# Second attention: row maxima turned in two halves, and only the first half ahead of the first score

## Chip, cores and metric

The kernel runs on one core of one Trainium2 chip. The metric is the device time of one execution in microseconds; three runs of the kernel before gave 2145.66, 2147.05 and 2149.94 us, median 2147.05. A difference of about 0.2% (4.3 us) is what a measurement of this kernel can tell from none.

## What is computed

Two transformer layers with adaptive layer norm. Each is an attention and a feed-forward part with a gated residual. Only the second layer's attention is touched: 32 heads of 16 dimensions, one key and one value head shared by all of them, causal, for 2 batches of 1024 tokens:

```python
q = (x @ wq).reshape(B, T, N_HEADS, HEAD_DIM)
k = x @ wk
v = x @ wv
scores = jnp.einsum('bqhd,bkd->bhqk', q, k) * scale
scores = jnp.where(causal[None, None], scores, -jnp.inf)
probs = jax.nn.softmax(scores.astype(jnp.float32), axis=-1)
out = jnp.einsum('bhqk,bkd->bqhd', probs, v).reshape(B, T, C)
```

The softmax subtracts the row maximum, which the kernel computes in a pass of its own.

## The kernel before

`attention1` is one block in which every engine runs its own written-out program; semaphores alone order them. It has 16 **steps** (`STEPS1`), one for each batch and group of 4 heads (`G`). A step has 12 **sets** (`QUADS`), the pairs of a half of the queries (`qc`, 512 of them) and a tile of 128 keys (`kt`) that the causal mask leaves: sets 0 to 3 belong to the first half of the queries, sets 4 to 11 to the second. In a set TensorE forms 4 score tiles, or 2 where two heads share one (sets 2, 3, 10 and 11), in three PSUM banks `scp` (`score`, L1770); ScalarE takes the exponential of each into `prob` (L1663). After each odd set TensorE multiplies the probabilities of two earlier sets with the values (`values`, L1817).

The negated row maximum enters a score as one more row of the queries (`MAXROW`), against a row of ones in the keys. So before a step's first score its maxima must be known. They come from a second pass over the same scores, in **units** (`maximum`, L1787 and L1792): a unit is 128 queries of a pair of heads against up to 512 keys, in one of two double banks `mxp`; VectorE reduces it (L1711 for a full unit, L1713 for one with the diagonal). A step has 24 units. Units 0 to 7 are the first four query tiles (256, 256, 512, 512, ... up to 1024 elements a row for both heads); units 8 to 23 the other four tiles, each with a full unit and a diagonal unit for both pairs of heads. After unit 23 VectorE joins the two parts (L1717). Then `turn_maxima` (L1805) transposes all maxima of the step on TensorE into the next `mxp` bank, ScalarE negates them into `mrow` (L1676), and SyncE moves them with 2 DMAs into the `MAXROW` rows of the step's query tile (L1612).

The order is written in numbers. 32 units (`LEAD`: the whole of step 0 and eight of step 1) and the turn of step 0 stand ahead of the first score. Then every set brings two units (`MQUAD`), so that step t's maxima are finished in set 7 of step t-1. They are turned at set 9 (`TURN_AT`), and TensorE waits for the row at set 0 of step t. A bank of `mxp` is free for its next user when VectorE has reduced the unit in it, or ScalarE has copied the turned maxima out of it (`freed`). In the last step no units are left, and `unread` (L1800) puts two matmuls that nobody reads in the place of each.

Of the kernel before, what the change touches and what calls it, by code (L numbers as in the profile page):

```python
# [17 lines left out]
P = 128  # L18
# [7 lines left out]
G = 4  # L26
# [1072 lines left out]
ATT1 = ("q_in2 q_in3 m_in0 m_in1 m_in2 m_in3 sc_ready exp_done pv_done u_copied mx_ready mx_done mx_joined "  # L1099
# [466 lines left out]

def max_banks():


    order = [("max", u) for u in range(LEAD)] + [("turn", 0)]  # L1570
    for q in range(QSETS):
        if q % QUADS == TURN_AT and q // QUADS + 1 < STEPS1:
            order.append(("turn", q // QUADS + 1))
        order += [("max", u) for u in range(LEAD + MQUAD * q, min(LEAD + MQUAD * (q + 1), MSTEP * STEPS1))]
    return {what: (i % MXBANKS, order[i - MXBANKS] if i >= MXBANKS else None) for i, what in enumerate(order)}


def attention1(nc, k, q_dram, sums, recips, stale, queries_in, next_loads, closed):

    with ExitStack() as ctx:  # L1580
# [5 lines left out]
        mxd, mxf = sb("mxd", [P, 2, 2, PAIRS, TILES]), sb("mxf", [P, 2, 2, PAIRS, TILES // 2])  # L1586
        mrow = sb("mrow", [G * TILES, 2, P], F32R)
# [5 lines left out]
        q_in, m_in = [s[f"q_in{i}"] for i in range(SLOTS1)], [s[f"m_in{i}"] for i in range(SLOTS1)]  # L1593
        MOVES = 16 * 3 * 2
        banks = max_banks()
        def freed(eng, what):
            before = banks[what][1]
            if before is not None and before[0] == "max":
                eng.wait_ge(s["mx_done"], before[1] + 1)
            if before is not None and before[0] == "turn":  # L1600
                eng.wait_ge(s["mrow_done"], before[1] + 1)

        with nc.Block() as block:
            @block.sync
            def _(sp):
# [27 lines left out]
                move(2)  # L1633
                next_loads(sp)
                maxima_row(0)
                for t in range(STEPS1):
                    if t >= 1:
                        if t + 3 < STEPS1:
                            sp.wait_ge(s["sc_ready"], SCORES1 * t)
                            move(t + 3)  # L1640
                        results(t - 1)
                    elif t + 3 < STEPS1:
                        move(t + 3)
                    if t + 1 < STEPS1:
                        maxima_row(t + 1)
                    if t >= 1:
                        reciprocals(t - 1)
# [4 lines left out]
            def _(act):  # L1652
# [19 lines left out]
                def maxima_out(t):  # L1672
                    act.wait_ge(s["mt_ready"], t + 1)
                    if t >= 2:
                        act.wait_ge(m_in[(t - 2) % SLOTS1], 32 * ((t - 2) // SLOTS1 + 1))
                    nc.scalar.activation(mrow[:, t % 2, :], mxp[banks["turn", t][0]][0:G * TILES, 0, 0:P], ACT.Copy, scale=-1.0).then_inc(s["mrow_done"], 1)  # L1676
                maxima_out(0)
                for t in range(STEPS1):
                    for n in range(QUADS):
                        if n == TURN_AT and t + 1 < STEPS1:  # L1680
                            maxima_out(t + 1)
# [21 lines left out]
            def _(dve):  # L1703
                def maximum(u):
                    t, (i, qt, part) = u // MSTEP, MPAIRS[u % MSTEP]
                    if u % MSTEP == 0 and t >= 2:
                        dve.wait_ge(s["mt_ready"], t - 1)
# [27 lines left out]
                for u in range(LEAD):  # L1735
                    maximum(u)
                for g in range(QSETS):
                    for u in range(LEAD + MQUAD * g, min(LEAD + MQUAD * (g + 1), MSTEP * STEPS1)):
# [9 lines left out]
            def _(pe):  # L1748
# [53 lines left out]
                def turn_maxima(t):  # L1802
                    pe.wait_ge(s["mx_joined"], t + 1)
                    freed(pe, ("turn", t))
                    nc.tensor.transpose(mxp[banks["turn", t][0]][0:G * TILES, 0, 0:P], mxd[:, t % 2].rearrange("p j i q -> p (j i q)"),  # L1805
# [379 lines left out]
```

## Time and profile before

| | us |
|---|---|
| median of 3 runs | 2147.05 |
| the profiled execution | 2148.23 |
| its span, first to last instruction | 2146.4 |
| TensorE busy in the span | 1964.6 (92%) |
| VectorE busy | 1174.6 (55%) |
| ScalarE busy | 903.1 (42%) |
| second attention, first unit to last values | 1462.9 to 2019 |

The profile's page gives busy times over the whole program. The second attention is read from its own windows and timelines. A window's row gives busy time for each engine and the mean clock granted to TensorE as a share of 2.4 GHz (0.50 is 1.2 GHz). Timelines give each instruction's start and length, and in brackets how long the engine sat idle before it and on whom. Matmuls overlap, so their lengths don't add up; distances between starts do.

### The profile page before, as it was taken

How to read it: one execution, taken by the hardware profiler on the slowest of the kernel's cores; microseconds unless marked ns; L12 is line 12 of the kernel's file. 1: busy time of each engine (PE TensorE's matmuls, PEld its weight loads, DVE VectorE, ACT ScalarE, POOL GpSimd, SP SyncE). 2: the span in 40 equal slices, each digit the busy share in tenths (PEclk: the TensorE clock that was granted, in tenths of full speed). 3: DMA queues.
4: the chain of work that ended last, by engine and by line, in shares of the span. 5: the costliest groups of instructions: out<-in, count | busy, mean ns of one | idle time of the engine just before them, and what ended most of it. 6: DMA issues, size and time to landing. Idle time of an engine off the chain costs nothing. (4 is left out here: it accounts for less than half of the span.)

```text
span 2146.4 us, 34674 instructions
## 1 busy us (share of the span) xinstructions
PE 1964.6 (92%) x12824; PEld 1177.3 (55%) x12824; DVE 1174.6 (55%) x2557; ACT 903.1 (42%) x1909; POOL 524.5 (24%) x408
## 2 busy tenths in 40 slices
PE   4859999999999999999986899997999999999698
PEld 4635666666666666666643454553444444444377
DVE  3536655555555555555401454446676767765078
ACT  2513344444444444444440122221666656656444
POOL 0014245555434444555330000000000000000143
PEclk8969999999999999999998999996999999999799
DMA  9742233222333233322236221144132222210121
GB/s 308 272 143 60 61 80 81 62 58 58 76 81 80 71 80 80 80 60 57 66 93 198 69 69 48 51 111 134 22 53 42 38 52 39 42 37 19 33 88 59
DMA packets 113594, 172.21 MB, mean 80 GB/s; under 512 B 26186, under 2 KB 46826, under 8 KB 113298
## 3 DMA queue, kind: packets, MB, share of 16 engines
q1 hardware_dynamic: 112402, 169.75, 29.8%
q8 instruction: 101, 1.65, 0.3%
q14 instruction: 67, 0.55, 0.1%
q10 hardware_dynamic: 1024, 0.26, 0.1%
HBM read 84.32 MB, written 29.38 MB: 53 GB/s over the span
## 5 line engine op out<-in xcount | busy, mean ns | idle before, releaser
L890 ACT ACTIVATE at_prob<-at_scp 128x512 f32<-128x512 f32 (+1 forms) x608 | 349.8, 576 | 515.4 <-PE at_scp L993 514.4
L1663 ACT ACTIVATE as_prob<-as_scp 128x512 f32<-128x512 f32 (+2 forms) x640 | 308.7, 564 | 197.5 <-PE as_scp L1773 148.2
L925 DVE CUSTOM_DVE_ANT_0 at_junk<-at_mxp,causal 128x128 f32<-128x128 f32 (+3 forms) x512 | 243.5, 488 | 190.5 <-PE at_mxp L1004 185.7
L1713 DVE TENSOR_REDUCE as_mxd<-as_mxp 128x2 f32<-128x256 f32 (+3 forms) x256 | 202.6, 820 | 98.3 <-PE as_mxp L1792 96.1
L920 DVE TENSOR_REDUCE at_mxf<-at_mxp 128x1 f32<-128x512 f32 x256 | 176.0, 688 | 143.4 <-PE at_mxp L1004 139.6
L1698 POOL TENSOR_TENSOR l_att_t<-l_att_t,as_spread 64x1024 f32<-64x1024 f32 x16 | 37.9, 2368 | 860.3 <-DMA as_spread<-l_recips 860.3
L820 POOL TENSOR_TENSOR at_pre<-at_prob 128x512 f32<-128x512 f32 x64 | 80.1, 1281 | 410.6 <-ACT at_prob L890 410.6
L1711 DVE TENSOR_REDUCE as_mxf<-as_mxp 128x2 f32<-128x1024 f32 x128 | 151.0, 1221 | 52.8 <-PE as_mxp L1787 52.6
L820 POOL TENSOR_TENSOR at_pre<-at_pre,at_prob 128x512 f32<-128x512 f32 x128 | 160.5, 1284 | 3.6 <-ACT at_prob L890 1.2
L1817 PE MATMUL as_op<-as_prob,l_vn 128*32 128x512 f32 (+3 forms) x1536 | 158.1, 533 | 0.3 <-ACT as_u_sb L1670 0.3
L989 PE MATMUL at_scp<-hd_early_q,l_khi 97*128 97x512 f32 (+1 forms) x304 | 138.3, 455 | 11.3 <-DMA hd_late_q<-at_slo 8.2
L1026 PE MATMUL at_op<-at_prob,l_cn 128*32 128x512 f32 (+3 forms) x1536 | 144.4, 493 | 4.0 <-ACT at_u_sb L861 4.0
L989 PE MATMUL at_scp<-at_qhi,l_khi 97*128 97x512 f32 (+1 forms) x304 | 138.7, 456 | 0.8 <-ACT at_prob L890 0.5
L1004 PE MATMUL at_mxp<-l_khi,hd_early_q 96*128 96x512 f32 (+2 forms) x384 | 126.2, 383 | 10.5 <-DMA hd_early_q<-at_shi 9.3
L1004 PE MATMUL at_mxp<-l_khi,at_qhi 96*128 96x512 f32 (+2 forms) x384 | 122.5, 367 | 0.5 <-DVE at_tm L950 0.2
L992 PE MATMUL at_scp<-hd_late_q,l_khi 96*128 96x512 f32 (+1 forms) x304 | 118.0, 388 | 0.0
L993 PE MATMUL at_scp<-hd_early_q,l_klo 96*128 96x512 f32 (+1 forms) x304 | 117.7, 387 | 0.0
L992 PE MATMUL at_scp<-at_qlo,l_khi 96*128 96x512 f32 (+1 forms) x304 | 116.8, 384 | 0.0
L993 PE MATMUL at_scp<-at_qhi,l_klo 96*128 96x512 f32 (+1 forms) x304 | 116.3, 383 | 0.0
L1787 PE MATMUL as_mxp<-l_keys,hd_early_q 48*128 48x512 f32 (+2 forms) x384 | 97.7, 488 | 19.2 <-DVE as_mxf L1711 7.3
L1770 PE MATMUL as_scp<-as_q,l_keys 49*128 49x512 f32 (+2 forms) x320 | 105.3, 444 | 7.4 <-ACT as_prob L1663 5.9
L1770 PE MATMUL as_scp<-hd_early_q,l_keys 49*128 49x512 f32 (+2 forms) x320 | 103.6, 445 | 5.7 <-ACT as_prob L1663 4.3
(250 smaller groups left out, 3494.4 us busy)
## 6 DMA issues: line engine op xcount, KB each, us to landing
hd_late_q<-at_slo SPq DMA_DIRECT2D x96, 128.0 KB, 2.4
at_qhi<-at_shi SPq DMA_DIRECT2D x96, 128.0 KB, 2.5
at_qlo<-at_slo SPq DMA_DIRECT2D x96, 128.0 KB, 2.4
hd_early_q<-at_shi SPq DMA_DIRECT2D x84, 128.0 KB, 2.4
at_spread<-l_recips SPq DMA_DIRECT2D x64, 128.0 KB, 2.7
l_o<-at_u_sb SPq DMA_DIRECT2D x16, 512.0 KB, 3.4
hd_early<-in_wmod SPq DMA_DIRECT2D x7, 1024.0 KB, 6.8
hd_late<-l_o SPq DMA_DIRECT2D x12, 512.0 KB, 4.1
```

The costliest lines, as they stand in the source:

```text
L820: nc.gpsimd.tensor_tensor(pre[:, j, :], other, prob[:, (x + j) % RING0, :], ALU.add).then_inc(s["pre_done"], 1)
L890: nc.scalar.activation(prob[:, x % RING0, c0:HALF], scp[x % BANKS0][:, c0:HALF], ACT.Exp).then_inc(s["exp_done"], 1)
L920: nc.vector.reduce_max(mxf[:, j, qt - 4:qt - 3], tile[:], AX_X).then_inc(s["mx_done"], 1)
L925: nc.vector.tensor_tensor_reduce(out=junk[:, u % 2, 0:w], in0=tile[:, 0:w], in1=k.causal[:, HALF - w:HALF], scale=1.0, scalar=LOWEST, op0= ...
L989: nc.tensor.matmul(out, k.khi[0:KR + 1, b, ks], q_cols(qhi[t % 2][0:KR + 1]), start=True, stop=False)
L992: nc.tensor.matmul(out, k.khi[0:KR, b, ks], q_cols(qlo[t % 2][0:KR]), start=False, stop=False)
L993: nc.tensor.matmul(out, k.klo[0:KR, b, ks], q_cols(qhi[t % 2][0:KR]), start=False, stop=True).then_inc(s["sc_ready"], 1)
L1004: nc.tensor.matmul(bank("max", t, u)[:, 0:w], qhi[t % 2][0:KR, qt // 4, j, qt % 4 * P:(qt % 4 + 1) * P], k.khi[0:KR, t // NG, k0:k0 + w], ...
L1663: nc.scalar.activation(prob[:, x % RING1, cols], scp[x % BANKS1][:, cols], ACT.Exp).then_inc(s["exp_done"], 1)
L1713: nc.vector.reduce_max(mxd[:, t % 2, :, i, qt:qt + 1], tile[:, :, 0:(qt % 4 + 1) * P], AX_X).then_inc(s["mx_done"], 1)
L1770: mm = nc.tensor.matmul(out, k.keys[rows, t // NG, kt * P:(kt + 1) * P], queries, start=True, stop=not diagonal)
L1817: mm = nc.tensor.matmul(op[2 * HD * j:2 * HD * (j + 1), c0:HALF], k.vn[:, t // NG, kt, :], prob[:, (x + j % UNITS1_OF[n]) % RING1, p0:p0 + ...
```

## The change

The 24 units keep their order. Only units 0 to 7 stand ahead of the first score; the turn, the negated copy and the move into the query tile are done for each half of the query tiles on its own. The first half's turn waits for eight units and stands at set 8 of the step before (`TURN_A1`); the second half's waits for the join and stands at set 1 of its own step, at set 3 in step 0 (`TURN_B1`). TensorE waits for a step's first half row at set 0, for its second half row at set 4. The lead over the sets shrinks from 32 units to 22. In step 0, sets 0, 1 and 2 carry 6, 6 and 8 units. A half row takes 4 DMAs of 4 x 128 elements, so a step has 8 in place of 2. On SyncE's queue the first half row goes ahead of the loads for the closing part (`next_loads`), and the second half row ahead of the results of the step before. In the last step `unread` begins at set 3.

```diff
-MPAIRS = [(i, qt, part) for qt in range(TILES) for part in range(1 + qt // 4) for i in range(PAIRS)]
+MPAIRS = [(i, qt, part) for half in range(2) for qt in range(4 * half, 4 * half + 4) for part in range(1 + half) for i in range(PAIRS)]
-LEAD = MSTEP + 8
-TURN_AT = 9
+FIRST_PAIRS = 4 * PAIRS
+LEAD = 22
+TURN_A1, TURN_B1 = 8, (3, 1)
...
+def pairs_ahead(g):
+    return FIRST_PAIRS + 6 * g if g < 3 else min(LEAD + MQUAD * g, MSTEP * STEPS1)
+
+def turns1(t, n):
+    return [(t, 1)] * (n == TURN_B1[min(t, 1)]) + [(t + 1, 0)] * (n == TURN_A1 and t + 1 < STEPS1)
...
-                def maxima_row(t):
-                    sp.wait_ge(s["mrow_done"], t + 1)
+                def maxima_row(t, half):
+                    sp.wait_ge(s["mrow_done"], 2 * t + half + 1)
                     for jj in range(2):
-                        sp.dma_start(words(q[t % SLOTS1][RG * jj + MAXROW:RG * jj + MAXROW + 1, :, :]),
-                                     words(mrow[jj * G * TILES // 2:(jj + 1) * G * TILES // 2, t % 2, :])).then_inc(m_in[t % SLOTS1], 16)
+                        for i in range(PAIRS):
+                            r = (jj * PAIRS + i) * TILES // 2
+                            sp.dma_start(words(q[t % SLOTS1][RG * jj + MAXROW:RG * jj + MAXROW + 1, i, HALF * half:HALF * (half + 1)]),
+                                         words(mrow[r:r + TILES // 2, t % 2, half, :])).then_inc(row_in[half][t % SLOTS1], 16)
...
                 move(2)
+                maxima_row(0, 0)
                 next_loads(sp)
-                maxima_row(0)
                 for t in range(STEPS1):
+                    if t >= 1 and t + 3 < STEPS1:
+                        sp.wait_ge(s["sc_ready"], SCORES1 * t)
+                        move(t + 3)
+                    maxima_row(t, 1)
                     if t >= 1:
-                        if t + 3 < STEPS1:
-                            sp.wait_ge(s["sc_ready"], SCORES1 * t)
-                            move(t + 3)
                         results(t - 1)
                     elif t + 3 < STEPS1:
                         move(t + 3)
                     if t + 1 < STEPS1:
-                        maxima_row(t + 1)
+                        maxima_row(t + 1, 0)
...
-                def turn_maxima(t):
-                    pe.wait_ge(s["mx_joined"], t + 1)
-                    freed(pe, ("turn", t))
+                def turn_maxima(t, half):
+                    if half == 0:
+                        pe.wait_ge(s["mx_done"], MSTEP * t + FIRST_PAIRS)
+                    else:
+                        pe.wait_ge(s["mx_joined"], t + 1)
+                    freed(pe, ("turn", t, half))
...
-                for u in range(LEAD):
+                for u in range(FIRST_PAIRS):
                     maximum(u)
-                turn_maxima(0)
+                turn_maxima(0, 0)
                 for g in range(QSETS):
                     t, n = divmod(g, QUADS)
-                    if n == TURN_AT and t + 1 < STEPS1:
-                        turn_maxima(t + 1)
-                    if n == 0:
-                        pe.wait_ge(m_in[t % SLOTS1], 32 * (t // SLOTS1 + 1))
-                    mine = range(LEAD + MQUAD * g, min(LEAD + MQUAD * (g + 1), MSTEP * STEPS1))
+                    for which in turns1(t, n):
+                        turn_maxima(*which)
+                    if n % 4 == 0 and n < 8:
+                        pe.wait_ge(row_in[n // 4][t % SLOTS1], ROWS * (t // SLOTS1 + 1))
+                    mine = range(pairs_ahead(g), pairs_ahead(g + 1))
                     for i in range(MQUAD):
-                        for u in mine[i:i + 1]:
+                        for u in mine[i * len(mine) // MQUAD:(i + 1) * len(mine) // MQUAD]:
                             maximum(u)
-                        if t == STEPS1 - 1:
-                            if n == 0 and i == 0:
+                        if t == STEPS1 - 1 and n >= 3:
+                            if n == 3 and i == 0:
                                 pe.wait_ge(s["mx_done"], MSTEP * STEPS1)
-                                pe.wait_ge(s["mrow_done"], STEPS1)
+                                pe.wait_ge(s["mrow_done"], 2 * STEPS1)
                             unread(t)
```

TensorE around the first turn and the first scores, of the kernel before (L1787 and L1792 are a unit, L1805 the turn, L1770 to L1773 a score; `hd_early_q` holds the queries):

```order
L1787 MATMUL as_mxp<-l_keys,hd_early_q 128x512 x2
L1792 MATMUL as_mxp<-l_tri 128x128 x4
L1805 MATMUL as_mxp<-ident,as_mxd 32x128
L1787 MATMUL as_mxp<-l_keys,hd_early_q 128x512 x2
L1770 MATMUL as_scp<-hd_early_q,l_keys 128x512
L1772 MATMUL as_scp<-l_tri 128x128
L1773 MATMUL as_scp<-l_tri 128x128
```

And of the changed kernel (L1805 and L1810 are a unit there, L1826 the turn, L1788 to L1791 a score):

```order
L1805 MATMUL as_mxp<-l_keys,hd_early_q 128x512 x2
L1810 MATMUL as_mxp<-l_tri 128x128 x4
L1826 MATMUL as_mxp<-ident,as_mxd 16x128
L1805 MATMUL as_mxp<-l_keys,hd_early_q 128x512 x4
L1805 MATMUL as_mxp<-l_keys,hd_early_q 128x256 x2
L1810 MATMUL as_mxp<-l_tri 128x128 x4
L1788 MATMUL as_scp<-hd_early_q,l_keys 128x512
L1790 MATMUL as_scp<-l_tri 128x128
L1791 MATMUL as_scp<-l_tri 128x128
```

The turn has 8 units ahead of it in place of 32 and takes half the columns; three units stand between it and the first score in place of one.

TensorE from the second unit of set 0 to the first of set 1 in a later step, before:

```order
L1787 MATMUL as_mxp<-l_keys,as_q 128x512 x2
L1770 MATMUL as_scp<-hd_early_q,l_keys 128x512
L1772 MATMUL as_scp<-l_tri 128x128
L1773 MATMUL as_scp<-l_tri 128x128
L1770 MATMUL as_scp<-hd_early_q,l_keys 128x512
L1772 MATMUL as_scp<-l_tri 128x128
L1773 MATMUL as_scp<-l_tri 128x128
L1787 MATMUL as_mxp<-l_keys,as_q 128x256 x2
L1792 MATMUL as_mxp<-l_tri 128x128 x4
```

The same place in the changed kernel:

```order
L1805 MATMUL as_mxp<-l_keys,hd_early_q 128x512 x2
L1810 MATMUL as_mxp<-l_tri 128x128 x4
L1788 MATMUL as_scp<-hd_early_q,l_keys 128x512
L1790 MATMUL as_scp<-l_tri 128x128
L1791 MATMUL as_scp<-l_tri 128x128
L1788 MATMUL as_scp<-hd_early_q,l_keys 128x512
L1790 MATMUL as_scp<-l_tri 128x128
L1791 MATMUL as_scp<-l_tri 128x128
L1826 MATMUL as_mxp<-ident,as_mxd 16x128
L1805 MATMUL as_mxp<-l_keys,as_q 128x256 x2
L1810 MATMUL as_mxp<-l_tri 128x128 x4
```

Set 0 now carries units 22 and 23, which have the diagonal, and the second half's turn stands between its last score and set 1, straight behind the unit whose reduction it waits for.

SyncE's queue up to the second row of maxima, before (L1120 loads queries, L1857 to L1862 are `next_loads`, L1612 is the row):

```order
L1120 DMA as_q<-scratch_queries 16x2x1024 x6
L1857 DMA hd_late<-in_wo 128x4x512
L1858 DMA hd_late<-scratch_w_feed 128x4x512
L1859 DMA l_bias<-in_b_base 128x512
L1862 DMA l_gates<-gate_rows 128x512 x4
L1612 DMA hd_early_q<-as_mrow 1x16x128 x2
L1120 DMA as_q<-scratch_queries 16x2x1024 x6
L1612 DMA hd_early_q<-as_mrow 1x16x128 x2
```

And of the changed kernel (L1627 is a half row):

```order
L1121 DMA as_q<-scratch_queries 16x2x1024 x6
L1627 DMA hd_early_q<-as_mrow 1x4x128 x4
L1878 DMA hd_late<-in_wo 128x4x512
L1879 DMA hd_late<-scratch_w_feed 128x4x512
L1880 DMA l_bias<-in_b_base 128x512
L1883 DMA l_gates<-gate_rows 128x512 x4
L1627 DMA hd_early_q<-as_mrow 1x4x128 x4
L1121 DMA as_q<-scratch_queries 16x2x1024 x6
L1627 DMA hd_early_q<-as_mrow 1x4x128 x4
```

The half row stands ahead of the closing part's loads, in 4 DMAs in place of 2.

## Rows read from the trace of the kernel before

**Rows 1.** Windows: us; busy us (x) of PE, PEld, DVE, ACT, POOL; clock; DMA.

```profile
1462.90:1494.50 31.60, 25.79 (x160) 13.54 (x160) 27.17 (x33) 0.00 (x0) 0.00 (x0) 0.50 0.48 134
...
1497.70:1509.80 12.10, 12.06 (x84) 7.61 (x84) 7.02 (x8) 5.93 (x12) 0.00 (x0) 0.52 0.35 65
...
1629.70:1661.30 31.60, 29.78 (x301) 15.40 (x297) 23.13 (x29) 20.21 (x43) 1.24 (x1) 1.00 0.24 41
1661.30:1694.60 33.30, 31.50 (x301) 15.60 (x297) 23.20 (x29) 20.20 (x43) 3.60 (x2) 0.95 0.27 47
1974.80:1984.20 9.40, 8.67 (x75) 3.80 (x71) 0.00 (x0) 5.53 (x13) 0.00 (x0) 1.00 0.14 35
```

**Rows 2.** Timeline of VectorE before the first score: start us, us, what.

```profile
1468.99 2.36 DVE L1713 TENSOR_REDUCE as_mxd<-as_mxp 128x2 f32<-128x1024 f32 x2 [0.27 <-PE as_mxp L1792]
...
1493.17 2.36 DVE L1713 TENSOR_REDUCE as_mxd<-as_mxp 128x2 f32<-128x1024 f32 x2 [0.27 <-PE as_mxp L1792]
```

**Rows 3.** Timeline of all engines, first turn of the maxima to the first score.

```profile
1494.54 0.37 PE L1805 MATMUL as_mxp<-ident,as_mxd 128*32 128x128 f32 x1 [0.55 <-DVE as_mxd L1713]
...
1495.24 1.17 SPq L1612 DMA_DIRECT2D hd_early_q<-as_mrow  x2
...
1497.72 0.80 PE L1787 MATMUL as_mxp<-l_keys,hd_early_q 48*128 48x512 f32 x2 [2.81 <-DMA hd_early_q<-as_mrow]
```

**Rows 4.** Groups of one shape over the second attention: busy us, mean ns, idle before.

```profile
L1711 DVE TENSOR_REDUCE as_mxf<-as_mxp 128x2 f32<-128x1024 f32 x128 | 151.0, 1221 | 52.8 <-PE as_mxp L1787 52.6
...
L1713 DVE TENSOR_REDUCE as_mxd<-as_mxp 128x2 f32<-128x1024 f32 x64 | 75.1, 1216 | 0.5 <-PE as_mxp L1792 0.5
L1713 DVE TENSOR_REDUCE as_mxd<-as_mxp 128x2 f32<-128x768 f32 x64 | 58.3, 952 | 34.5 <-PE as_mxp L1792 34.5
...
L1713 DVE TENSOR_REDUCE as_mxd<-as_mxp 128x2 f32<-128x512 f32 x64 | 43.3, 689 | 17.9 <-PE as_mxp L1792 15.8
...
L1713 DVE TENSOR_REDUCE as_mxd<-as_mxp 128x2 f32<-128x256 f32 x64 | 27.1, 423 | 45.4 <-PE as_mxp L1792 45.3
```

**Rows 5.** Timeline of TensorE: set 8 of step 4, sets 0 to 3 of step 5.

```profile
1650.37 0.38 PE L1787 MATMUL as_mxp<-l_keys,as_q 48*128 48x256 f32 x2
...
1661.35 0.50 PE L1787 MATMUL as_mxp<-l_keys,as_q 48*128 48x512 f32 x2
...
1663.17 0.38 PE L1787 MATMUL as_mxp<-l_keys,as_q 48*128 48x256 f32 x1
...
1665.30 0.86 PE L1817 MATMUL as_op<-as_prob,l_vn 128*32 128x256 f32 x16
1666.09 0.50 PE L1787 MATMUL as_mxp<-l_keys,as_q 48*128 48x512 f32 x2
...
1667.91 0.39 PE L1787 MATMUL as_mxp<-l_keys,as_q 48*128 48x256 f32 x2 [0.61 <-DVE as_mxf L1711]
...
1669.48 1.71 PE L1817 MATMUL as_op<-as_prob,l_vn 128*32 128x512 f32 x16
```

**Rows 6.** Timeline of VectorE, step 5: units 8 and 9, then 22, 23 and the join.

```profile
1661.89 2.36 DVE L1711 TENSOR_REDUCE as_mxf<-as_mxp 128x2 f32<-128x1024 f32 x2 [0.53 <-PE as_mxp L1787]
...
1678.60 2.35 DVE L1713 TENSOR_REDUCE as_mxd<-as_mxp 128x2 f32<-128x1024 f32 x2
1680.97 0.18 DVE L1717 TENSOR_TENSOR as_mxd<-as_mxd,as_mxf 128x16 f32<-128x16 f32 x1
```

**Rows 7.** Timeline of TensorE, last step: set 2 and the values after set 3.

```profile
1988.79 0.39 PE L1800 MATMUL as_mxp<-l_keys,as_q 48*128 48x256 f32 x2
...
1991.46 1.71 PE L1817 MATMUL as_op<-as_prob,l_vn 128*32 128x512 f32 x16 [0.34 <-ACT as_u_sb L1670]
```

**Rows 8.** Windows: dense stretch at the start, and around one fall of the clock.

```profile
1502.00:1508.00 6.00, 5.99 (x45) 4.05 (x45) 4.11 (x5) 3.38 (x8) 0.00 (x0) 0.50 0.01 3
...
1676.00:1680.00 4.00, 3.66 (x24) 1.90 (x22) 3.68 (x4) 3.51 (x9) 0.00 (x0) 0.99 0.00 0
1680.00:1683.00 3.00, 3.00 (x17) 0.59 (x16) 1.12 (x2) 1.12 (x3) 0.00 (x0) 0.50 0.00 0
```

More of the change, by code:

```diff
@@ L1564, in _ @@
                             split_keys(g)
+def pairs_ahead(g):
+    return FIRST_PAIRS + 6 * g if g < 3 else min(LEAD + MQUAD * g, MSTEP * STEPS1)
+def turns1(t, n):
+    return [(t, 1)] * (n == TURN_B1[min(t, 1)]) + [(t + 1, 0)] * (n == TURN_A1 and t + 1 < STEPS1)
 def max_banks():
-    order = [("max", u) for u in range(LEAD)] + [("turn", 0)]
+    order = [("max", u) for u in range(FIRST_PAIRS)] + [("turn", 0, 0)]
     for q in range(QSETS):
-        if q % QUADS == TURN_AT and q // QUADS + 1 < STEPS1:
-            order.append(("turn", q // QUADS + 1))
-        order += [("max", u) for u in range(LEAD + MQUAD * q, min(LEAD + MQUAD * (q + 1), MSTEP * STEPS1))]
+        order += [("turn", *which) for which in turns1(*divmod(q, QUADS))]
+        order += [("max", u) for u in range(pairs_ahead(q), pairs_ahead(q + 1))]
     return {what: (i % MXBANKS, order[i - MXBANKS] if i >= MXBANKS else None) for i, what in enumerate(order)}
@@ L1592, in attention1 @@
         op = ps("op", [P, HALF])
-        q_in, m_in = [s[f"q_in{i}"] for i in range(SLOTS1)], [s[f"m_in{i}"] for i in range(SLOTS1)]
+        q_in = [s[f"q_in{i}"] for i in range(SLOTS1)]
+        row_in = [[s[f"{name}{i}"] for i in range(SLOTS1)] for name in ("m_in", "m_late")]
+        ROWS = 16 * 2 * PAIRS
         MOVES = 16 * 3 * 2
@@ L1600, in freed @@
             if before is not None and before[0] == "turn":
-                eng.wait_ge(s["mrow_done"], before[1] + 1)
+                eng.wait_ge(s["mrow_done"], 2 * before[1] + before[2] + 1)
         with nc.Block() as block:
@@ L1670, in copy_out, with maxima_out @@
                     nc.scalar.activation(u_sb[:, t % 2, HALF * hf:HALF * (hf + 1)], op[:], ACT.Copy).then_inc(s["u_copied"], 1)
-                def maxima_out(t):
-                    act.wait_ge(s["mt_ready"], t + 1)
+                def maxima_out(t, half):
+                    act.wait_ge(s["mt_ready"], 2 * t + half + 1)
                     if t >= 2:
-                        act.wait_ge(m_in[(t - 2) % SLOTS1], 32 * ((t - 2) // SLOTS1 + 1))
-                    nc.scalar.activation(mrow[:, t % 2, :], mxp[banks["turn", t][0]][0:G * TILES, 0, 0:P], ACT.Copy, scale=-1.0).then_inc(s["mrow_done"], 1)
-                maxima_out(0)
+                        act.wait_ge(row_in[half][(t - 2) % SLOTS1], ROWS * ((t - 2) // SLOTS1 + 1))
+                    nc.scalar.activation(mrow[:, t % 2, half, :], mxp[banks["turn", t, half][0]][0:G * TILES // 2, 0, 0:P], ACT.Copy, scale=-1.0).then_inc(s["mrow_done"], 1)
+                maxima_out(0, 0)
                 for t in range(STEPS1):
                     for n in range(QUADS):
-                        if n == TURN_AT and t + 1 < STEPS1:
-                            maxima_out(t + 1)
+                        for which in turns1(t, n):
+                            maxima_out(*which)
                         exps(t, n)
@@ L1706, in maximum @@
                     if u % MSTEP == 0 and t >= 2:
-                        dve.wait_ge(s["mt_ready"], t - 1)
+                        dve.wait_ge(s["mt_ready"], 2 * t - 3)
+                    if u % MSTEP == FIRST_PAIRS and t >= 2:
+                        dve.wait_ge(s["mt_ready"], 2 * t - 2)
                     tile = mxp[banks["max", u][0]]
@@ L1734, in split_weights @@
                     nc.vector.tensor_tensor(low[:, c, :], whole[:, c, :], high[:, c, :].bitcast(F32), ALU.subtract).then_inc(s["w_lo"], 1)
-                for u in range(LEAD):
+                for u in range(FIRST_PAIRS):
                     maximum(u)
                 for g in range(QSETS):
-                    for u in range(LEAD + MQUAD * g, min(LEAD + MQUAD * (g + 1), MSTEP * STEPS1)):
+                    for u in range(pairs_ahead(g), pairs_ahead(g + 1)):
                         maximum(u)
@@ L1800, in unread @@
                         nc.tensor.matmul(tile[:, jj, 0:2 * P], q[t % SLOTS1][rows, 0, 0:P], k.keys[rows, t // NG, 0:2 * P], start=True, stop=True)
[L1802 to L1805 removed]
+                def turn_maxima(t, half):
[4 more added lines that the diff above has]
+                    freed(pe, ("turn", t, half))
+                    nc.tensor.transpose(mxp[banks["turn", t, half][0]][0:G * TILES // 2, 0, 0:P], mxd[:, t % 2, half].rearrange("p j i q -> p (j i q)"),
                                         k.ident[:]).then_inc(s["mt_ready"], 1)
```

14 lines of the change are left out of this document (7 added, 7 removed).

## The prediction

> **What bounds the kernel now.** I read the windows of the second attention first. A whole step of 31.6 us (step 4) has TensorE busy for 29.78, VectorE for 23.13, ScalarE for 20.21, at clock 1.00; step 5 took 33.3 us at 0.95 [rows 1]. So in the steps TensorE is the bound by its own order, with short waits on the two others. Ahead of them lies a stretch of another kind: for 34.8 us (1462.9 to 1497.7) no score is formed. In its first 31.6 us VectorE is busy for 27.17 and the clock is 0.50 [rows 1]; the last 3 us go to the turn and the row. The reader is to see that VectorE reducing 32 units sets the pace there. Next I read when unit 7 is reduced (1468.99 + 2.36 = 1471.35, for units 6 and 7 together) and when the last of the lead is (1495.53) [rows 2], and the chain from the turn to the first score: turn at 1494.54, two DMAs issued from 1495.24 to 1496.41, TensorE going on at 1497.72, so 0.70 us to the issue, 0.585 for each DMA and 1.31 after the last [rows 3].
>
> **The head.** The first turn can start when unit 7 is reduced, at about 1471.4. The issue starts at 1472.1; four DMAs take 4 x 0.585 = 2.34 instead of 1.17, and 1.31 more lands the half row at 1475.8, against 1497.7. This is no gain of 22 us, since 24 units are only moved behind it. Sets 0 to 2 carry 20 units, 8 to 27. VectorE needs for them 8 x 1.221 for the full ones, 2 x (1.216 + 0.952 + 0.689 + 0.423) = 6.56 for the diagonal ones of the second half, 0.18 for the join and 2 x (0.423 + 0.689) = 2.22 for units 24 to 27, together 18.7 us [rows 4]. It was busy for 27.17 of 31.60 us in the lead, 88% after the first 0.9 us; at that share the 18.7 take 21.2 us, and with the first unit coming at 1476.5 they end at 1497.7. The ten scores of these sets fit beside. TensorE may begin set 3 a little sooner, near 1497.2. Sets 0 to 3 with their values took 12.1 us before at clock 0.52 [rows 1]; set 3 and the values are about 5 of it. Set 4 then begins at 1502.2 in place of 1509.8: a gain of 7.6 us. The second half row, turned at the start of set 3, lands 0.70 + 2.34 + 1.31 = 4.4 us later, just under those 5. Bounds: 5.5 (the waits of both engines add up more than in the lead, or the row is late) and 9.5 (the clock rises before set 3, and only the row, at about 1501, is waited for).
>
> **Steps 1 to 14, sets 0 and 1.** Here is what the change adds each time. Units 22 and 23 now stand in set 0, and the second half's turn right behind it; it waits for the join. Queued behind it on TensorE are units 0 and 1 and the four scores of set 1, and ScalarE, which has done set 0 by then, waits for these. In step 5 set 0 began at 1661.35 and set 1 at 1663.17, 1.82 us later [rows 5]. VectorE began the first of set 0's units 0.54 after its start and needed 2.35 for units 22 and 23 together, then 0.18 for the join [rows 6]. With the diagonal's matmuls 0.1 later this gives 0.64 + 2.35 + 0.18 = 3.2 us after the set's start. TensorE has its four scores by 2.1 (1.82 and two diagonals), so it stands for 1.1 us, and with 0.2 for the turn set 1 begins at 3.4 instead of 1.82: 1.6 late. Set 1 took 2.13 (to 1665.30) [rows 5], partly behind the exponentials of set 0, which no longer queue: 0.4 back. I take +1.2. Bounds +0.4 (only the turn and the diagonals, if the reductions are further ahead than in this row) and +1.6.
>
> **Sets 2 and 3** take from 1666.09 to 1669.48, 3.39 us, of which TensorE waits 0.61 for the reduction of a full unit [rows 5]. They now carry units 2 to 5, whose reductions take 0.42 to 0.95. The nearest row is the last step, in which unread matmuls stand there: from 1988.79 to 1991.46, 2.67 us, ended by the copy of the output on ScalarE [rows 7]. I take -0.7; the bounds are 0 and -0.8.
>
> **The other sets.** Full and diagonal units change places. In sets 4 to 9 the exponentials of 4 x 512 columns pace the scores, and a diagonal costs 0.1 where it comes ahead of the first score. Sets 10 and 11 win about 0.1 by full units. The first half's turn stands at set 8 with 6 later units behind its last one, so nothing waits. Together 0, between -0.2 and +0.3. The DMAs: 8 for 2 is 3.5 us of issue a step on SyncE. The half row for set 4 is issued at the start of set 1 and needs 4.4 us; sets 1 to 3 with values take over 6. Were that cover gone, TensorE would stand at set 4 for what is over. The results behind it on the queue wait for the output copy of set 2 anyway, the other half row has sets 8 to 11 (11 us), and the query load stands ahead as before. All nothing.
>
> A step is so 1.2 - 0.7 = +0.5 us, 14 steps +7.0, with bounds -0.3 and +1.5 for one step.
>
> **The end.** Sets 8 to 11 of step 14 had no units and took 9.4 us (1974.8 to 1984.2) [rows 1]; with units they take 1661.35 - 1650.37 = 11.0 [rows 5]: +1.6. Step 15 pays the wait of set 0 (+1.2) and saves at most 0.2 where sets 0 to 2 lose their unread matmuls: +1.0. Bounds for both 1.5 and 4, since without unread matmuls the clock may fall sooner.
>
> **Sum.** -7.6 + 7.0 + 1.6 + 1.0 = +2.0 us on the profiled execution's 2148.23, so 2150.2. That execution is 1.2 above the median of the runs, so 2149.0.
>
> **The clock.** Fine windows show seven stretches at half clock in steps 1 to 14, one in every second step: after 4 us in which TensorE was busy for 3.66, the next 3 us ran at 0.50 [rows 8]. One costs 1.7 us (33.3 against 31.6) [rows 1]. I leave their number at seven. But sets 6 and 7, behind which they fall, now stream fewer columns (units 10 to 13 instead of 20 to 23), and the new stand in set 0 is a second weak place.
> The Trainium skill (TensorE: Matmul & The Clock Gate, What's actually happening) says that the clock drops after an idle window and rises under sustained matmuls. The trace does not agree: here it fell after a stretch without such a gap, and in the head it stayed at 0.50 through 6.00 us of which TensorE was busy for 5.99 [rows 8]. By the page a stand of 1.1 us adds no fall, the sum stays at 2149, and the denser head would rise early, which would give 2147.
>
> **Rivals.**
> *The steps come out even or better* (27%). TensorE stands behind ScalarE in most sets, so part of the 1.2 us may be won back in sets 1 to 3. At 0 a step the sum is 2142, at -0.3 and a head of 9.5 it is 2136. For it: VectorE has 8.5 us free a step. Against: the join can't come before two reductions of 1.2 us that start in set 0.
> *More falls of the clock* (20%), slower. If the weak place of set 6 and 7 or of set 0 is met in every step, seven further stretches at 1.7 us add 12: 2161; three add 5: 2154. It decides from two on. For it: fewer columns there, and a stand; against: the falls came only in every second step.
> *The wait is dearer* (14%), slower. If VectorE enters set 0 with unit 21 undone, or nothing comes back in sets 1 to 3, a step costs +1.3: 14 x 0.8 = 11 more, 2160. It decides from +0.7 a step.
> *The change doesn't shorten the head* (3%): if the row or VectorE makes sets 0 to 3 as long as the lead was, +8: 2157.
> My own sum has 36%.
>
> **The numbers.** 0.2%, 4.3 us, is about what a measurement of this kernel can tell from none. My sum and the smaller versions of the rivals lie inside 2142.8 to 2151.3. Faster: 0.28, nearly all of it the first rival. Slower: 0.35, the second, third and fourth less their mild forms, with a part of mine. Same: 0.37. The range is 2139 to 2161: it leaves out the best head with gaining steps, and the clock together with a dear wait. The likeliest case alone has 2144 to 2154.
>
> **What would show it.** In the new trace: the first score within 1478 to 1480 (right) and set 4 of step 0 near 1502; a wait of TensorE on the join of about 1 us before 15 of the second turns; sets 2 and 3 in about 2.7 us; half-clock stretches in every second step. I am wrong if that wait is under 0.4 or over 1.6, if set 4 begins outside 1500 to 1505, or if the clock falls in most steps.

## The result, and the profile after

The changed kernel takes 2170.96 us (median of 4 runs, 2169.97 to 2172.64) against 2146.36 for the one before (4 runs): ratio 1.0117, 95% interval 1.0105 to 1.0129. It is 24.6 us slower. The forecast was 2149.0 with a range of 2139 to 2161; the time lies outside it.

Four windows of the second attention tell where the time went: to set 4 of step 0, the rest of step 0, steps 1 to 14, step 15. Their columns are those of [rows 1]. Before the change:

```profile
1462.90:1509.80 46.90, 38.23 (x245) 21.25 (x245) 35.22 (x41) 7.48 (x14) 0.00 (x0) 0.51 0.42 107
1509.80:1531.60 21.80, 20.97 (x203) 10.42 (x199) 15.20 (x17) 14.27 (x30) 0.00 (x0) 1.00 0.06 15
1531.60:1984.20 452.60, 426.85 (x4116) 215.54 (x4112) 312.27 (x372) 282.93 (x602) 30.83 (x13) 0.97 0.23 40
1984.20:2018.90 34.70, 32.94 (x252) 16.21 (x248) 0.35 (x1) 19.86 (x42) 4.72 (x2) 0.80 0.09 17
```

After it:

```profile
1461.40:1500.50 39.10, 30.08 (x204) 15.96 (x204) 26.22 (x31) 7.48 (x15) 0.00 (x0) 0.50 0.43 118
1500.50:1525.70 25.20, 24.69 (x187) 11.81 (x183) 15.54 (x16) 14.29 (x30) 0.00 (x0) 0.78 0.18 28
1525.70:2003.90 478.20, 448.55 (x4176) 224.59 (x4172) 322.09 (x381) 285.48 (x616) 31.41 (x14) 0.95 0.22 38
2003.90:2042.20 38.30, 36.06 (x253) 16.86 (x249) 3.03 (x5) 20.38 (x43) 4.12 (x2) 0.73 0.08 16
```

| part (to the hundredth from the timelines) | before | after | change |
|---|---|---|---|
| first unit to set 4 of step 0 | 46.87 | 39.11 | -7.8 |
| sets 4 to 11 of step 0 | 21.72 | 25.21 | +3.5 |
| steps 1 to 14 | 452.6 | 478.2 | +25.6 |
| step 15 to the end of its values | 34.8 | 38.3 | +3.5 |

The head gave what was forecast (7.6), and steps 1 to 14 gave back more than three times as much. The four changes add up to +24.9 us; the two traced executions are 23.0 us apart (spans of 2169.4 and 2146.4), since the attention began 1.6 us earlier and what follows it took 0.3 us less. The head's chain, a timeline of all engines, answers to [rows 3]:

```profile
1469.78 0.38 PE L1826 MATMUL as_mxp<-ident,as_mxd 128*16 128x128 f32 x1 [1.59 <-DVE as_mxd L1731]
...
1470.49 2.54 SPq L1627 DMA_DIRECT2D hd_early_q<-as_mrow  x4
...
1474.11 1.22 PE L1805 MATMUL as_mxp<-l_keys,hd_early_q 48*128 48x512 f32 x4 [3.95 <-DMA hd_early_q<-as_mrow]
...
1476.81 0.77 PE L1788 MATMUL as_scp<-hd_early_q,l_keys 49*128 49x512 f32 x2
```

The turn comes at 1469.78 (the attention begins at 1461.36 here, 1.6 us earlier than in the trace before), the half row takes four DMAs in 2.54 us, TensorE stands for 3.95 us, and the first score is formed at 1476.81, 15.5 us after the first unit instead of 35.

One step, TensorE's timeline, set 0 to the values after set 3 (answers to [rows 5]):

```profile
1696.52 0.49 PE L1805 MATMUL as_mxp<-l_keys,as_q 48*128 48x512 f32 x2
...
1699.81 0.28 PE L1826 MATMUL as_mxp<-ident,as_mxd 128*16 128x128 f32 x1 [0.89 <-DVE as_mxd L1735]
1700.01 0.39 PE L1805 MATMUL as_mxp<-l_keys,as_q 48*128 48x256 f32 x2
...
1702.02 0.86 PE L1838 MATMUL as_op<-as_prob,l_vn 128*32 128x256 f32 x16
1702.80 0.39 PE L1805 MATMUL as_mxp<-l_keys,as_q 48*128 48x256 f32 x2
```

```profile
1705.66 1.71 PE L1838 MATMUL as_op<-as_prob,l_vn 128*32 128x512 f32 x16
```

and VectorE's beside it (answers to [rows 6]):

```profile
1697.18 2.36 DVE L1731 TENSOR_REDUCE as_mxd<-as_mxp 128x2 f32<-128x1024 f32 x2 [0.53 <-PE as_mxp L1810]
1699.58 0.18 DVE L1735 TENSOR_TENSOR as_mxd<-as_mxd,as_mxf 128x16 f32<-128x16 f32 x1
```

The turn at 1699.81 has waited 0.89 us for the join of 1699.58. The chain is the forecast one: the step's units 22 and 23 are reduced in 2.36 us from 1697.18 on, and nothing else can go in front. It stands in all 15 of these turns (13.2 us in total, 0.88 or 0.89 each). Sets 0 and 1 took 5.50 us (1696.52 to 1702.02) against 3.95, sets 2 and 3 2.86 (1702.80 to 1705.66) against 3.39.

Steps 1 to 13 of the kernel before took 33.25 and 31.63 us in turn (within 0.01), the longer ones with one stretch at half clock. After the change each of the fourteen takes 34.13 to 34.17 us, and each has such a stretch, behind sets 6 and 7. Windows around one:

```profile
1679.00:1682.00 3.00, 2.31 (x12) 0.99 (x9) 2.14 (x3) 3.00 (x7) 0.00 (x0) 1.00 0.00 0
1682.00:1686.00 4.00, 4.00 (x18) 0.83 (x18) 0.65 (x1) 1.38 (x3) 0.00 (x0) 0.57 0.00 0
```

TensorE was busy for 2.31 of the 3.00 us ahead of the fall: in sets 6 and 7 it stands behind ScalarE, and its units there are now small (10 and 11 have 256 keys).

### The profile page after: what moved, and what is told of

Read it like the earlier page. It is cut to its first block and busy times, and to the rows that moved or that the text cites. A ratio compares the mean times of both kernels' runs of the same rounds, so it can differ in the third digit from the quotient of the medians.

```text
span 2169.4 us, 34858 instructions
## 1 busy us (share of the span) xinstructions
PE 1983.1 (91%) x12828; PEld 1180.3 (54%) x12828; DVE 1178.9 (54%) x2557; ACT 906.1 (42%) x1925; POOL 524.6 (24%) x408
## 5 line engine op out<-in xcount | busy, mean ns | idle before, releaser
L1838 PE MATMUL as_op<-as_prob,l_vn 128*32 128x512 f32 (+3 forms) x1536 | 172.7, 575 | 2.1 <-ACT as_u_sb L1686 0.8
L1788 PE MATMUL as_scp<-as_q,l_keys 49*128 49x512 f32 (+2 forms) x320 | 115.4, 465 | 7.1 <-ACT as_prob L1679 5.9
L1788 PE MATMUL as_scp<-hd_early_q,l_keys 49*128 49x512 f32 (+2 forms) x320 | 114.2, 471 | 6.1 <-ACT as_prob L1679 5.0
L1805 PE MATMUL as_mxp<-l_keys,hd_early_q 48*128 48x512 f32 (+2 forms) x384 | 101.3, 474 | 13.7 <-PEq L1220 4.7
```

What stands on the lines that cost most here:

```text
L1788: mm = nc.tensor.matmul(out, k.keys[rows, t // NG, kt * P:(kt + 1) * P], queries, start=True, stop=not diagonal)
L1838: mm = nc.tensor.matmul(op[2 * HD * j:2 * HD * (j + 1), c0:HALF], k.vn[:, t // NG, kt, :], prob[:, (x + j % UNITS1_OF[n]) % RING1, p0:p0 + ...
```

## The experiments

Every run has its median beside the kernel before on the same chip. For steps 1 to 14 I also give what a full step without half clock in it takes (the **clean step**; those of one trace agree within 0.05), and what the fourteen took over 14 clean steps (the **clock's cost**). A **fall** is a stretch at half clock. The clock's cost comes from one traced execution for each kernel. Before: 31.63 us, and 452.6 + 1.6 (step 14 lacked eight units) - 442.8 = 11.4. After: no step is clean. The runs were made on three chips, on which the kernel before took 2147.03, 2147.47 and 2146.47 us, so medians of different chips can be set side by side to about 1 us.

The theories: the **stand** (the wait on the join is a loss in every step), **columns** (the clock falls because sets 6 and 7 now stream fewer of them), and **length** (the clock falls at intervals that the length of a step decides).

**1. The second turn one set later.**

```diff
-TURN_A1, TURN_B1 = 8, (3, 1)
+TURN_A1, TURN_B1 = 8, (3, 2)
```

> The changed kernel with the second half's turn at set 2 instead of set 1 (step 0 stays at set 3); all else the same. Three theories of the 24.6 us. Stand: TensorE's wait of 0.88 us for the join at set 1 is a real loss in each of 15 steps; then it goes, with what ScalarE and set 1 lose behind it, 0.9 to 1.5 us a step, 13 to 20 us. Columns: the clock falls in every step because sets 6 and 7 now stream fewer columns; then a half-clock stretch stays in every one of steps 1 to 14, a step takes about 33.2 us and the time is 2156 to 2159. Length: the clock falls where a fall is due by the length of a step; with the step back near 31.7 us at full clock it falls in every second step, as before the change, and the time is 2145 to 2148. If the stand was only taken from waits that come later anyway, the time stays over 2168.

Measured: 2147.35 us (10 runs), ratio to before 1.0001 (0.9991 to 1.0010). The windows of its steps 1 to 14 and of one clean step (set 8 to set 8), then TensorE's timeline with sets 0 and 1, the turn, and the values after set 3:

```profile
1521.60:1981.90 460.30, 444.86 (x4176) 231.19 (x4172) 320.83 (x381) 284.82 (x616) 31.57 (x14) 0.94 0.23 39
1708.90:1740.30 31.40, 30.14 (x303) 15.98 (x299) 23.36 (x28) 20.30 (x44) 2.37 (x1) 1.00 0.27 46
```

```profile
1719.54 0.50 PE L1805 MATMUL as_mxp<-l_keys,as_q 48*128 48x512 f32 x2
...
1723.67 0.86 PE L1838 MATMUL as_op<-as_prob,l_vn 128*32 128x256 f32 x16
1724.46 0.28 PE L1826 MATMUL as_mxp<-ident,as_mxd 128*16 128x128 f32 x1
...
1727.52 1.71 PE L1838 MATMUL as_op<-as_prob,l_vn 128*32 128x512 f32 x16 [0.15 <-ACT as_u_sb L1686]
```

One number moved, and 23.6 us went. By the traces about 16 of them are the clean step (14 x 1.2), 3.2 the last step (38.3 to 35.1); 3.5 lie in step 0, whose instructions are the same in both kernels (more on this under *The edges*). The wait of 0.9 is gone, sets 0 and 1 take 4.13 us, sets 2 and 3 with the turn 3.06 (1724.46 to 1727.52). A clean step is 31.37 us, 0.26 less than before the change. But the clock costs 460.3 - 439.2 = 21.1 us, so the length theory (2145 to 2148) has the time right by luck and the reason wrong: there are nine falls, five behind sets 6 and 7 and four behind sets 4 and 5 that last 10 us. What the stand cost is shown; that the clock's cost hangs on it is refuted.

**2. A lead of 32 units**, the order of units in the steps as before the change.

```diff
-LEAD = 22
+LEAD = 32
```

> The changed kernel with a lead of 32 units instead of 22: the short head and the two turns stay, but in steps 1 to 15 every set carries the units that it carried before the change (8 and 9 in set 0, 20 to 23 in sets 6 and 7), and 22 and 23 are reduced half a step ahead of the second turn. Stand theory: no wait on the join is left, 0.9 to 1.5 us a step less. Columns theory: sets 6 and 7 stream as many columns as before, so the clock falls in every second step again; with both, a step takes 31.8 at full clock and the time is 2148 to 2153 (two turns cost 2 to 3 us in all, and sets 0 to 2 of step 0 carry 30 units, so the head gives its 7.8 us back). If the two turns or the 8 DMAs themselves cost the time, it stays over 2160.

Measured: 2176.91 us, ratio 1.0131 (1.0116 to 1.0146). The stand and columns theories are both wrong on it; the outcome named last, over 2160 if the turns or the DMAs themselves cost the time, has come. Its set 4 of step 0 begins 49.9 us after the first unit (39.1 in the changed kernel), and its steps take 34.1 us each, all with a fall. The timeline of all engines at sets 0 and 1 shows why:

```profile
1671.77 0.50 PE L1805 MATMUL as_mxp<-l_keys,as_q 48*128 48x512 f32 x2
...
1672.39 2.36 DVE L1729 TENSOR_REDUCE as_mxf<-as_mxp 128x2 f32<-128x1024 f32 x2 [0.60 <-PE as_mxp L1805]
...
1673.94 0.28 PE L1826 MATMUL as_mxp<-ident,as_mxd 128*16 128x128 f32 x1
...
1674.80 0.39 PE L1805 MATMUL as_mxp<-l_keys,as_q 48*128 48x256 f32 x2 [0.58 <-DVE as_mxf L1729]
```

The turn takes one of only two banks while the full units 8 and 9 are being reduced (2.36 us for both). The unit behind it needs the other bank and waits for VectorE: it starts 0.86 us after the turn and 3.03 after the set (1671.77 to 1674.80), 0.58 of it idle. The pair of sets took 5.03 us instead of 3.95. A turn at set 1 is dear even where its own input is ready. Sets 6 and 7 carried the units of the kernel before here, and yet the clock fell in each step; so columns there alone don't decide how often.

**3. Units 10 to 13 doubled, the stand kept.** In this and all "doubled" runs the first matmuls of the named units are issued twice into the same bank:

```diff
-                    for jj in range(2):
+                    twice = u % MSTEP in (10, 11, 12, 13)
+                    for again, jj in [(a, j) for a in range(1 + twice) for j in range(2)]:
...
-                                              ..., start=True, stop=full)
+                                              ..., start=True, stop=full or again < twice)
```

> The changed kernel with the score matmuls of units 10 to 13 (sets 6 and 7 of steps 1 to 14) issued twice into the same bank: 8 more matmuls a step of 256 or 512 columns, where ScalarE paces the scores. The stand in set 0 stays. Columns theory: sets 6 and 7 are no longer thin, the half-clock stretch after them goes in most or all steps; each is worth 1.65 us, so minus 11 to 23 us, 2148 to 2160. Length theory: falls come as often as before, and the doubled matmuls cost 0 to 0.5 us a step: 2171 to 2178.

Measured: 2185.89 us, ratio 1.0175 (1.0159 to 1.0191): slower by another 15 us. Windows of steps 1 to 14, of the stand at set 0 and what follows, and of the place where the falls had been:

```profile
1521.60:2019.10 497.50, 473.54 (x4288) 252.29 (x4284) 323.00 (x381) 287.16 (x616) 31.65 (x14) 0.88 0.21 36
1664.00:1666.00 2.00, 1.11 (x11) 0.55 (x7) 1.86 (x3) 1.85 (x4) 0.00 (x0) 1.00 0.94 137
1666.00:1673.00 7.00, 7.00 (x67) 4.59 (x67) 2.23 (x5) 3.09 (x8) 0.00 (x0) 0.56 0.03 6
1685.00:1688.00 3.00, 3.00 (x34) 1.22 (x35) 0.87 (x2) 1.24 (x3) 0.00 (x0) 1.00 0.03 5
```

Its clean step is 32.66 us. In this step, step 5, the fall behind sets 6 and 7 is gone (1685 to 1688 at 1.00). But TensorE, busy for 1.11 of 2.00 us around the stand, fell to half clock within 1 us of the turn (0.56 is the mean of the 7 us). Eleven of the fourteen steps show a stretch that begins within 2 us of the second turn; none shows one behind sets 6 and 7, and four show one of 10 us behind sets 4 and 5. The clock's cost rose to 497.5 - 457.2 = 40.3 us. With these units doubled, the stand is a second place from which the clock falls.

**4. The kernel before with units 20 and 21 doubled (set 6).**

```diff
+                    twice = u % MSTEP in (20, 21)
```

> The kernel before the change with the matmuls of the full units 20 and 21 (set 6) issued twice into the same bank, 4 more of 512 columns a step. Columns theory: the seven half-clock stretches after set 7 go, seven times 1.65 us: about 2135. Length theory: they stay, seven of them, and the time is 2146 to 2150.

Measured: 2155.48 us (10 runs), ratio 1.0037 (1.0023 to 1.0052). Neither number came: not the gain of 11 us of the columns theory, not the 2146 to 2150 of the length theory. A clean step grew to 31.86, 3.2 us in all, and the clock cost 460.0 + 1.6 - 446.0 = 15.6 instead of 11.4. Of nine falls four begin behind sets 4 and 5, three still behind sets 6 and 7, two behind sets 8 and 9. Covering one thin place did not take the falls away.

**5. No stand, units 10 to 13 doubled.** The two edits of 1 and 3.

> The second turn at set 2 (no stand in set 0) and the matmuls of units 10 to 13 (sets 6 and 7) issued twice: against the run with the same doubling and the stand (2185.9) only the stand differs, against the run with the turn at set 2 alone (2147.4) only the doubling. If the stand is a second place from which the clock falls, beside thin sets, then the stretches of 6.8 us right behind set 0's stand go, together with 1.3 us a step of waiting: under 2150. Falls behind sets 6 and 7 should be gone, those behind sets 4 and 5 remain: 2135 to 2147. If doubling by itself brings falls, the time is over 2155.

Measured: 2136.52 us, ratio 0.9956 (0.9942 to 0.9970). Steps 1 to 14:

```profile
1523.40:1974.20 450.80, 435.41 (x4288) 233.74 (x4284) 320.95 (x381) 284.54 (x616) 31.24 (x14) 0.97 0.24 40
```

A clean step is 31.49 us, the clock costs 450.8 - 440.9 = 9.9. Five falls are left of run 1's nine: four behind sets 6 and 7 (run 1: five), one behind sets 4 and 5 (run 1: four). So what went are mostly the long ones that began ahead of the doubled units. The expectation had it the other way round. Against run 3 only the stand differs: 49 us, of which 16 are the clean step and 30 the clock. Against run 1 only the doubling: -11.

**6. The same with units 8 to 13 doubled.**

> The same with units 8 to 13 doubled, so that sets 5, 6 and 7 all stream more columns and no stand is left. If thin sets are the cause of falls, few are left in steps 1 to 14, a step is near its 31.4 to 31.6 us at full clock and the time is 2127 to 2137, below both kernels. If falls are set by the length of a step or are bound to come at some rate, it is 2145 or more.

Measured: 2133.73 us, ratio 0.9950 (0.9934 to 0.9967). Steps 1 to 14:

```profile
1520.40:1967.00 446.60, 430.70 (x4346) 235.45 (x4342) 320.85 (x381) 286.44 (x616) 33.16 (x14) 0.99 0.24 41
```

Eleven of fourteen steps are clean at 31.53 to 31.56; the clock costs 446.6 - 441.7 = 4.9 us. The three falls left all begin behind sets 6 and 7. This trace is of the fastest of the five executions, 4.1 us under their median, so 4.9 is a favourable figure.

**7. A lead of 24 units**, units 22 and 23 in set 11, the turn at set 1.

```diff
-LEAD = 22
+LEAD = 24
```

> The changed kernel with a lead of 24 units: units 22 and 23 stand in set 11 of the step before, the second half's turn stays at set 1, set 2 of step 0 carries two units more. If the 1.3 us a step come from the wait for a reduction that was just issued, they go: no wait on the join, a step at full clock near 31.4, and the time is 2145 to 2152. If they come from a turn at set 1 as such (its bank, ScalarE's copy in front of set 1's exponentials), a good part stays: over 2158.

Measured: 2168.22 us, ratio 1.0112 (1.0088 to 1.0136). Steps 1 to 14:

```profile
1530.50:2012.60 482.10, 454.34 (x4176) 227.49 (x4172) 320.55 (x381) 289.13 (x616) 31.51 (x14) 0.91 0.22 38
```

The wait on the join is gone, the time is not. Sets 0 and 1 took 4.44 us, and sets 10 and 11, which now carry units 20 to 23, 3.51 against 2.93 in the changed kernel: four units of 1.2 us of reduction each in sets with two scores. Two of the steps have no fall and take 31.95 us (in the changed kernel 32.55, in run 1 31.37), the rest have stretches at half clock (0.91 on average), and the clock costs 482.1 - 447.3 = 34.8 us. The traced execution is the slowest of four, 6.7 us over their median. So the forecast "over 2158" for a turn at set 1 that costs as such came true, but for another reason in the main: of the 1.2 us a step half came back, sets 0 and 1 are 0.3 us longer than with the turn at set 2 (4.13), the moved units cost 0.6 in sets 10 and 11, and the rest is the clock.

**8. The kernel before with 16, 17, 20 and 21 doubled (sets 4 and 6).**

> The kernel before with the full units of sets 4 and 6 (16, 17, 20, 21) doubled. With set 6 alone doubled the stretches at half clock moved from behind set 7 to behind set 5 and the time rose to 2155. If thin sets are the cause, both places are covered now: fewer than seven stretches in steps 1 to 14 and 2136 to 2144. If more matmuls bring more falls, 2155 or more.

Measured: 2152.65 us, ratio 1.0033 (1.0020 to 1.0046). In the trace the clock's cost is 456.1 + 1.6 - 449.5 = 8.2 us, five stretches for seven, but a clean step takes 32.11, 0.48 more than before. Over all executions the granted clock is 0.949, against 0.9485 for the kernel before on this chip, so a gain by the clock is not shown. The matmuls cost more than they save. Why a doubled set costs 0.23 us here and 0.12 in run 5 is not shown; that the full units of sets 4 and 6 hold up scores that ScalarE waits for is my guess.

**9. Units 6 to 13 doubled, no stand.**

> The turn at set 2 and units 6 to 13 doubled, so that sets 4 to 7 all stream more columns. In the run with units 8 to 13 doubled (2133.7) four stretches at half clock were left in steps 1 to 14 (three of 3.4 us, one of 10.2). If set 4's columns are what is left of the cause, they go: minus 3 to 8 us, 2126 to 2131. Doubling itself lengthens sets 4 and 5 by up to 0.1 us a step, 1.4 us. If the last falls have another cause, 2133 to 2136.

Measured: 2136.49 us, ratio 0.9955 (0.9940 to 0.9970), not told apart from run 6. Two falls are left in steps 1 to 14, both behind sets 6 and 7, but a clean step takes 31.76. Past run 6 the filler costs what it saves.

**10. Run 6, and unread matmuls of 512 columns in the last step.**

```diff
-                        nc.tensor.matmul(tile[:, jj, 0:2 * P], ..., k.keys[rows, t // NG, 0:2 * P], start=True, stop=True)
+                        nc.tensor.matmul(tile[:, jj, 0:4 * P], ..., k.keys[rows, t // NG, 0:4 * P], start=True, stop=True)
```

> The run with units 8 to 13 doubled, and in the last step the unread matmuls with 512 columns instead of 256. The last step spends 20.5 us at half clock from its set 4 on. If too few columns in its sets bring that about, most of it goes and the step is 5 to 9 us shorter: 2125 to 2130. If it is the values at half clock and the waits on ScalarE, nothing changes or it is 1 to 3 us longer: 2134 to 2137.

Measured: 2132.22 us, ratio 0.9939 (0.9919 to 0.9960). The last step:

```profile
1972.10:2006.10 34.00, 29.35 (x253) 14.46 (x249) 3.00 (x5) 20.60 (x44) 2.37 (x2) 0.99 0.12 22
```

The window reaches 3 us past the last values. Its clock is 0.99; the changed kernel's last step has 0.73. The expectations of runs 9 and 10 misread run 6's trace: its stretch of 10.2 us at half clock lies in the last step and not in steps 1 to 14, and the one of 20.5 us begins 3 us behind the last step's values, where run 10 still has it. From its start to the start of its last values it takes 28.5 us against 31.0 in run 6. The whole kernel gained 1.5 us, less than the runs' spread. It has the lowest median of this study, 0.6% ahead of the kernel before.

**Side by side.** The granted clock is the mean over the whole program, median of all executions of the kernel; falls, clean step and clock's cost are of steps 1 to 14 in the one trace.

| kernel | us | granted clock | falls | clean step | clock's cost |
|---|---|---|---|---|---|
| before | 2146.36 | 0.948 | 7 | 31.63 | 11.4 |
| changed | 2170.96 | 0.9405 | 14 | 32.55 (derived below) | 22.5 |
| 1, turn at set 2 | 2147.35 | 0.941 | 9 | 31.37 | 21.1 |
| 3, 10 to 13 doubled, stand | 2185.89 | 0.9285 | 15 | 32.66 | 40.3 |
| 4, before, 20 and 21 doubled | 2155.48 | 0.9455 | 9 | 31.86 | 15.6 |
| 5, turn at set 2, 10 to 13 doubled | 2136.52 | 0.950 | 5 | 31.49 | 9.9 |
| 6, turn at set 2, 8 to 13 doubled | 2133.73 | 0.952 | 3 | 31.55 | 4.9 |
| 7, lead 24 | 2168.22 | 0.938 | 12 | 31.95 | 34.8 |
| 8, before, 16, 17, 20, 21 doubled | 2152.65 | 0.949 | 5 | 32.11 | 8.2 |

How much chance is in one trace, runs 6 and 10 show: their instructions are the same up to the last step, and the traces have three and five falls in steps 1 to 14 (446.6 and 449.8 us). So 7 falls against 9 or 5 (before, runs 4 and 8) tell little by themselves; 7 against 14, and 9 against 5 and 3, are borne out by the granted clock of all executions.

## Why the prediction was wrong

*The head* was right: -7.6 forecast, -7.8 measured, by the steps given (half row after 4.3 us, set 4 at 39.1 us after the first unit, forecast 39.2).

*The wait on the join* was right as a mechanism and nearly as a size: 1.1 us forecast, 0.89 measured. What hangs on it was mis-sized. I took back 0.4 us because set 1 would no longer queue behind ScalarE; set 1 took 2.01 us from its unit (1700.01 to 1702.02), against 2.13, so only 0.12 came back. Sets 0 and 1 cost +1.55 and not +1.2.

*Sets 2 and 3*: -0.7 forecast, -0.53 measured. The last step's row that I used has unread matmuls with no diagonals, and was too cheap a model for units 2 to 5.

*The other sets*: 0 forecast, -0.1 measured. Sets 4 and 5 took 4.04 against 3.87, sets 6 and 7 4.42 (in run 1, with the same units) against 4.35; sets 8 to 11 gained 0.34 (4.22 against 4.44, and 2.92 against 3.05). A clean step of the changed kernel is 32.66 less the 0.11 that doubling costs (run 5 against run 1), 32.55, against 31.63: +0.9 a step, 12.9 us in fourteen, where the sum had +0.5 and 7.0. The 0.4 between them is the term of sets 0 and 1 (0.35) and that of sets 2 and 3 (0.17), less 0.1. Run 1 shows that the stand accounts for 32.55 - 31.37 = 1.2 us of it, more than the whole difference.

*The clock* is the step that failed. "I leave their number at seven" was wrong: it fell in all fourteen. The clock's cost in steps 1 to 14 is 478.2 - 14 x 32.55 = 22.5 us against 11.4, +11.1, near the +12 of the rival that I gave 20%. Without these 11 us the time would have been 2160, inside the range. The condition named there, fewer columns in sets 6 and 7, has support: with the units there doubled the fourteen falls behind these sets are gone (run 3), and without the stand the clock's cost goes from 21.1 to 9.9 and, with set 5 filled as well, to 4.9 (runs 1, 5, 6). It is not proven as the cause of the doubling from seven to fourteen: runs 5 and 6 keep four and three falls behind the filled sets 6 and 7, and run 2 falls there in every step with the units of the kernel before. The other condition, the stand, is no cause of the fourteen falls (they all begin behind sets 6 and 7, and run 1 has nearly the same cost without a stand), but the clock does fall behind it where sets 6 and 7 are filled (run 3), and once in the changed kernel, in step 15.

*The edges.* The rest of step 0 cost 3.5 us, forecast 0: a stretch of 10 us at half clock (0.78 on average in the second window above) that is not in the trace before. It is not in the trace of run 1 either, whose instructions in step 0 are those of the changed kernel one for one; so the order of the work in step 0 does not by itself bring this fall. Step 15 cost 3.5, forecast 1.0, at clock 0.73 against 0.80. The unread matmuls that sets 1 and 2 lack are not the main cause of it, since run 1 lacks them too. The rest of step 0 and step 15 of run 1:

```profile
1499.88:1521.63 21.75, 20.82 (x186) 10.15 (x183) 15.53 (x16) 14.21 (x30) 0.00 (x0) 0.99 0.19 32
1981.92:2017.04 35.12, 33.49 (x253) 16.15 (x249) 3.02 (x5) 20.23 (x43) 3.92 (x2) 0.81 0.09 18
```

Its step 15 takes 35.1 us at 0.81, close to the kernel before. So most of the 3.5 us goes with the stand: the wait, and a stretch at half clock that begins 5.9 us into the step and that run 1 does not have. With step 14's 1.6 the two make 5.1, over the upper bound of 4.

So of +24.9 us in the second attention about 12.9 are the longer clean step, 11 the clock in steps 1 to 14, 1.6 the units of step 14, 7 the edges, less 7.8. Against the forecast of +2.0 that is 22.9 us missed: 11 by the number of falls, 6 by the clean step, 6 by the edges. What went wrong in weighing is that I priced two rivals apart, the dearer wait (+11) and the clock (+12), which both came true in part at the same time, and cut the range at either alone.

The Trainium skill's rule weighed in the prediction (TensorE: Matmul & The Clock Gate, What's actually happening: the clock drops after an idle window) would have given no new falls. The trace shows fourteen where there had been seven; the one opened above came after a stretch in which TensorE was busy for 2.31 of 3.00 us. In run 3 the clock also fell behind the stand of 0.9 us.

Open: why the same stand brings a fall behind it in run 3 and none in steps 1 to 14 of the changed kernel; why run 2, with sets 6 and 7 as in the kernel before, falls in every step; and why the same instructions of step 0 run with a fall in one trace and without one in another. In the changed kernel and in run 2 the steps are 34.1 to 34.2 us long with one fall in each; whether this length keeps the falls coming was not separated from the rest. So that the clock fell twice as often is shown, and why it did is not.

## What to carry to other kernels

An instruction that waits for a reduction should stand a set behind the unit that feeds it, not right behind it: one number was worth 1.2 us in each of 14 steps. Moving work out of a head changes what stands beside what in every later step, so each step is to be walked through set by set, banks included. Where TensorE stands behind another engine, its clock is a cost of its own to be budgeted: matmuls that nobody needs, put where another engine paces, gained 0.5 to 0.7% over run 1 here (runs 5, 6 and 10), and lost 0.3 to 0.4% in the kernel before (runs 4 and 8) and 0.7% beside a stand (run 3). So they are to be measured in place, each time.

## What was not expected of the hardware

- Steps of the changed kernel repeat to 0.04 us (34.13 to 34.17), fall included; the kernel before repeats in pairs (33.26 and 31.63 us).
- More matmuls made a kernel faster: run 6 issues 12 more a step than run 1 (4346 against 4176 in the windows of steps 1 to 14, some records missing) and is 13.6 us faster, as its clock's cost is lower (4.9 against 21.1 us in the traces, 0.952 against 0.941 granted over all executions).
- In run 3 the clock was 0.56 on average over 7 us behind a stand of 0.9 us, while TensorE was busy for 7.00 of 7.00 us.
- The same instructions of step 0 took 25.2 us at 0.78 in the trace of the changed kernel and 21.75 at 0.99 in that of run 1.
